# Cross-attention and gated FFN block: activations transposed by SP's DMAs instead of TensorE

## The reference

```
x = x + tanh(g_xattn) * attention(layernorm(x), ctx)   # 32 query heads of width 16, 8 key/value heads
x = x + tanh(g_ffn)   * ffn(layernorm(x))              # 512 -> 1536 -> 512

attention: q = X Wq^T + bq;  k, v = ctx Wk^T + bk, ctx Wv^T + bv
           softmax(q k^T / 4, masked by rows and by padding) v, then Wo, bo
ffn:       (silu(X gate_w * gate_s) * (X up_w * up_s)) down_w * down_s, weights rounded to fp8
```

## Time and profile before

| | |
|---|---|
| median of 3 runs | 626.36 us (625.19 to 628.47) |
| the profiled execution | 625.76 us, span 624.0 us |
| mean granted clock of PE | 0.967 of full |
| busy: PE, DVE, ACT, POOL | 572.9, 494.7, 361.4, 236.6 us |
| DMA | 50.24 MB, mean 81 GB/s |

### The profile page before, as it was taken

One profiled execution on the slowest core, in us unless ns is written; L12 is line 12 of the kernel. 1 busy time (PEld: TensorE's weight loads), 2 busy tenths in 40 slices (PEclk: granted clock), 3 DMA queues, 4 the chain that ended last, 5 costly groups with the idle time before them and its releaser, 6 DMA issues.

```text
span 624.0 us, 14382 instructions
## 1 busy us (share of the span) xinstructions
PE 572.9 (92%) x5165; PEld 358.2 (57%) x5165; DVE 494.7 (79%) x1527; ACT 361.4 (58%) x672; POOL 236.6 (38%) x323
## 2 busy tenths in 40 slices
PE   4747798699999999999999999999998999799997
PEld 4525353357764677457755776467744664466683
DVE  3577667989889999998989988998799888754321
ACT  4453577457674567546664668366755664675361
POOL 3020204020465117630565038611652266038383
PEclk9958899779999999999999999999999999999999
DMA  8683564433021501233121412120323010020000
GB/s 290 210 269 110 162 149 133 122 97 124 14 58 29 177 4 46 69 93 104 29 72 39 124 45 59 49 77 27 79 51 89 3 30 8 19 71 20 17 19 34
DMA packets 53872, 50.24 MB, mean 81 GB/s; under 512 B 7501, under 2 KB 41386, under 8 KB 53802
## 3 DMA queue, kind: packets, MB, share of 16 engines
q1 hardware_dynamic: 53280, 48.72, 26.9%
q10 hardware_dynamic: 522, 0.61, 0.3%
HBM read 35.15 MB, written 9.44 MB: 71 GB/s over the span
## 4 chain that ended last, share of the span: by engine, by line
PE 74%; DVE 15%; issue 4%; DMA 2%; POOL 2%; ACT 1%; SPq 0%; ACTq 0%; POOLq 0%; DVEq 0%
PE work L1178 28%; PE work L1189 10%; PE av L1078 8%; PE work L1109 7%; DVE junk L896 6%; PE sc L1052 6%; PE sc L1068 4%; PE work L1156 4%; DVE ws L905 4%; PE work L1129 2%; PE sc L1064 1%; PE work L1165 1%; PE work L1139 1%; PE work L1118 1%; DVE bst L837 1%
## 5 line engine op out<-in xcount | busy, mean ns | idle before, releaser
L896 DVE CUSTOM_DVE_ANT_0 junk<-sc,mq 128x256 bf16<-128x256 f32 x512 | 186.4, 420 | 40.7 <-PE sc L1052 39.2
L905 DVE SCALAR_TENSOR_TENSOR ws<-sc,padc,mask_k 128x1024 f32<-128x1024 f32 x112 | 143.3, 1280 | 11.8 <-PE sc L1068 9.1
L762 ACT ACTIVATE ws<-ws 128x1024 f32<-128x1024 f32 x112 | 116.2, 1052 | 17.0 <-DVE ws L905 16.8
L691 POOL TENSOR_TENSOR ff<-ga,up 128x256 f32<-128x256 f32 x96 | 69.3, 730 | 113.2 <-DVE ga L986 112.8
L1178 PE MATMUL work<-h_h,wg 128*128 128x256 f16 x384 | 89.6, 274 | 2.0 <-DVE h_l L981 2.0
L1178 PE MATMUL work<-h_h,wu 128*128 128x256 f16 x384 | 89.1, 273 | 0.0
L1178 PE MATMUL work<-h_l,wu 128*128 128x256 f16 x384 | 89.0, 273 | 0.0
L1178 PE MATMUL work<-h_l,wg 128*128 128x256 f16 x384 | 89.0, 273 | 0.0
L698 POOL TENSOR_TENSOR f_l<-ff,f_h 128x256 f16<-128x256 f32 x96 | 63.9, 672 | 56.4 <-ACT f_h L828 56.3
L1189 PE MATMUL work<-wd,f_h 128*128 128x512 fp8e4 x192 | 73.0, 380 | 0.0
L1189 PE MATMUL work<-wd,f_l 128*128 128x512 fp8e4 x192 | 72.8, 379 | 0.0
(11 more groups left out here) (129 smaller groups left out, 1029.9 us busy)
## 6 DMA issues: line engine op xcount, KB each, us to landing
qs<-q_scratch SPq DMA_DIRECT2D x96, 64.0 KB, 2.5
cin<-in_ctx SPq DMA_DIRECT2D x8, 512.0 KB, 4.2
xin<-in_x SPq DMA_DIRECT2D x8, 512.0 KB, 5.4
xb<-in_x SPq DMA_DIRECT2D x8, 512.0 KB, 4.3
att_u<-un SPq DMA_DIRECT2D x128, 32.0 KB, 2.0
out_x<-yt SPq DMA_DIRECT2D x16, 256.0 KB, 2.0
ks<-k_scratch SPq DMA_DIRECT2D x48, 64.0 KB, 2.5
q_scratch<-qh SPq DMA_DIRECT2D x16, 128.0 KB, 2.0
```

Source lines behind the costliest of these rows:

```text
L691: pool.tensor_tensor(ff[:, n % RING, :], ga[:, n % RING, :], up[:, n % RING, :], ALU.mult).then_inc(ff_done, 1)
L762: act.activation(ws[:, unit, :, :], ws[:, unit, :, :], ACT.Exp, scale=1.0 / SSC).then_inc(exp_done, 1)
L896: last = dve.tensor_tensor_reduce(junk[:, j, :], sc[0][:, place(j)], mq[b % 2][:, t, :], 1.0, -3.4e38, ALU.add, ALU.max, mx[:, t, col:col ...
L905: dve.scalar_tensor_tensor(out=ws[:, n % 4, :, :], in0=sc[1][:, :].rearrange("p (j l) -> p j l", j=HPG), scalar=padc[b % 2][:, kt:kt + 1], ...
```

## The change

The three activations are split into high and low halves first, with rows on the partitions, and then each half is transposed by a DMA of SP.

- PE: `xT`, `cT`, `x2T` go, 24 transposes of 128x128 f32 in a batch; with them six uses of the PSUM banks.
- ACT: the cast to the high half now reads the f32 rows in SBUF and writes a row tile (xr_h, cr_h, h2r_h), 128x512, for each half n of the rows.
- POOL: the subtraction to the low half (xr_l, cr_l, h2r_l), six of 128x512 in a batch, in place of DVE's six.
- SP: twelve `dma_start_transpose` of 128x512 f16 in a batch (four each for x, c, x2), from the row tiles into xh, xl, ch, cl, h2_h, h2_l. The low one waits for POOL behind the high one.
- Waits: q waits for x_in, k (and with it v) for c_in, gu for h2_in, each 64 for four transfers. The loads of x and c wait for POOL's subtraction of the batch before. SP waits, before it overwrites xh, ch or h2_h, for the last reader on PE (q 1, v, gu 11 of the batch before).
- Tiles: xn and x2n go; the norms write xin and xb in place, so the residual's load of the next batch waits for x2_low. mask_b and ident_b lie in yt. The factor 4 of ctx goes into Wk.
- All places are set anew. From the second out of batch 3 to its first gu, PE now has

```diff
-IN_BANKS = ("xT", "q", "cT", "k", "v", "spread", "out", "x2T", "gu")
+IN_BANKS = ("q", "k", "v", "spread", "out", "gu")
...
                 if name == "load_x" and b:
-                    sp.wait_ge(normed[0], 2 * b)
+                    sp.wait_ge(x_low, 2 * b)
...
                 if name == "load_xb":
+                    past(sp, x2_low, 2 * b)
+                    sp.dma_start(xb[:, :, :], x_v[b]).then_inc(ld_xb, 16)
+                if name == "xT":
+                    sp.wait_ge(x_high, 2 * b + n + 1)
                     if b:
-                        wait_free(sp, "out", 1, b - 1)
-                    sp.dma_start(xb[:, :, :], x_v[b]).then_inc(ld_xb, 16)
+                        wait_ready(sp, "q", 1, b - 1)
+                    sp.dma_start_transpose(xh[:, :, n * P:(n + 1) * P], xr_h[:, n, :]).then_inc(x_in, 16)
+                    sp.wait_ge(x_low, 2 * b + n + 1)
+                    sp.dma_start_transpose(xl[:, :, n * P:(n + 1) * P], xr_l[:, n, :]).then_inc(x_in, 16)
...
+                if name == "x2T":
+                    pool.wait_ge(x2_high, 2 * b + n + 1)
+                    past(pool, h2_in, 64 * b)
+                    pool.tensor_tensor(h2r_l[:, n, :], xb[:, n, :], h2r_h[:, n, :],
+                                       ALU.subtract).then_inc(x2_low, 1)
...
                 if name == "x2T":
-                    wait_ready(act, name, n, b)
-                    if b:
-                        wait_ready(act, "gu", FT - 1, b - 1)
-                    act.activation(h2_h[:, 2 * n:2 * n + 2, :], halves(bank), ACT.Copy).then_inc(x2_high, 1)
+                    act.wait_ge(normed[1], 2 * b + n + 1)
+                    past(act, h2_in, 64 * b)
+                    act.activation(h2r_h[:, n, :], xb[:, n, :], ACT.Copy).then_inc(x2_high, 1)
...
-                if name == "x2T":
-                    dve.wait_ge(x2_high, 2 * b + n + 1)
-                    dve.tensor_tensor(h2_l[:, 2 * n:2 * n + 2, :], halves(bank), h2_h[:, 2 * n:2 * n + 2, :],
-                                      ALU.subtract).then_inc(freed, 1)
...
                 if name == "gu":
                     if n == 0 and b == 0:
                         pe.wait_ge(f8_done, len(slabs))
                     if n == 0:
-                        for i in range(2):
-                            wait_free(pe, "x2T", i, b)
+                        pe.wait_ge(h2_in, 64 * (b + 1))
```

More of the change, by code:

```diff
@@ L53 @@
 PE_AT = {
[L54 to L60, removed]
@@ L117 @@
[L117 to L125, removed]
+    "pad_row": [3.2532],
+    "padc": [37.6401],
@@ L126 @@
+    "x2T": [98.4415, 99.1556],
 }
 SP_AT = {
[L129 to L139, removed]
+    "load_x": [-200.8497],
+    "load_c": [-188.9527],
+    "load_xb": [-92.1274],
+    "put_q": [-158.3097, -136.9484],
@@ L140 @@
+    "get_q": [-156.1422, -130.376],
+    "rows": [-125.4718, -108.2147],
+    "gather": [-95.302, -92.1126],
+    "store": [-28.1756, -26.6447],
+    "put_k": [-157.9372],
+    "get_k": [-146.8456],
+    "den": [-92.1957],
+    "xT": [-175.9939, -173.1422],
+    "cT": [-170.0178, -168.223],
+    "x2T": [-70.2614, -69.3271],
 }
 PE_FIRST = {
-    "gu": [50.2422, 53.1248, 54.0185, 55.067, 56.535, 58.2144, 58.704, 59.2703, 59.342, 59.8342, 62.2681, 62.4752],
-    "maxima": [-183.727, -50.8962, -23.9023, -17.9854, -17.7211, -17.69, -17.3057, -13.7715, -6.7207, -2.2685,
-               -0.4092, 0.9104, 2.1701, 2.5303, 6.5651, 7.8774],
@@ L208 @@
+    "cT": [-9944.6745, -9903.0438],
+    "x2T": [102.8167, 103.3011],
 }
 SP_FIRST = {
-    "load_xb": [-76.7724],
-    "put_q": [-201.5747, -106.2388],
-    "get_q": [-138.1748, -103.8086],
-    "rows": [-100.2596, -77.6096],
-    "gather": [-70.3549, -50.0156],
-    "store": [-10.7445, -1.7046],
-    "put_k": [-139.0221],
-    "get_k": [-137.4682],
-    "den": [-65.5708],
+    "load_xb": [-126.6719],
+    "put_q": [-154.9186, -142.2669],
+    "get_q": [-148.04, -140.3164],
+    "rows": [-126.827, -104.8412],
@@ L292 @@
+    "cT": [-24.2735, -22.0353],
+    "x2T": [92.3431, 92.938],
 }
 SP_LAST = {
-    "load_x": [-165.1293],
-    "load_c": [-160.3978],
-    "load_xb": [-73.5065],
-    "put_q": [-129.106, -123.6214],
-    "get_q": [-111.2559, -107.6974],
-    "rows": [-105.2968, -81.0932],
-    "gather": [-75.6883, -59.0669],
-    "store": [-40.8265, -40.7234],
-    "put_k": [-138.4836],
-    "get_k": [-125.9663],
-    "den": [-65.2771],
+    "load_x": [-214.721],
+    "load_c": [-204.6784],
+    "load_xb": [-99.5857],
@@ L305 @@
+    "put_q": [-161.6389, -154.4471],
+    "get_q": [-154.2496, -129.2075],
+    "rows": [-124.753, -116.3198],
+    "gather": [-97.8443, -75.8103],
+    "store": [-49.5226, -49.197],
+    "put_k": [-157.672],
+    "get_k": [-153.7618],
+    "den": [-88.4027],
+    "xT": [-172.6298, -168.3597],
+    "cT": [-185.1658, -177.3801],
+    "x2T": [-72.5445, -69.4743],
 }
 SETUP = ["columns", "Wk", "Wq0", "Wq1", "Wq2", "Wq3", "Wv", "mask", "Wo0", "Wo1", "Wo2", "Wo3"]
-SETUP_PE = [-5352.6902, -5349.489, -5174.4074, -5165.6533, -5156.8993, -5139.3911, -4544.8103, -997.1066,
-    -988.8414, -653.6282, -261.8989, -220.8964]
```

469 lines of the change are left out of this document (236 added, 233 removed).

## The result

Twenty executions of the changed kernel on the same chips as twenty of the kernel before: **623.09 us** (621.16 to 629.71) against 627.59 us (625.19 to 633.25), ratio **0.9933, 95% interval 0.9912 to 0.9954** (below, the brackets behind a ratio are this interval). The change gains 0.7% where 2.1% was forecast. The profiled execution took 621.2 us, its span is 619.4 (before 625.76 and 624.0). Single executions of either kernel spread over 8 us, and the kernel before's four longest of the seventeen timed beside e1 to e4 (630.7 to 632.7 us) had a granted clock of 0.951 to 0.957, the other thirteen 0.965 to 0.970.

A forecast was written before the change was run, and what follows sets the result against it. PE was taken to bound the steady state, with the fill setting the pace before. Span 624.0 - 16.2 (transposes) + 2.0 (head) + 1.4 (tail) = 611.2, plus 1.8 around it: 613 us, -2.1%; range 601 to 655.

The forecast's parts named there:

- the head: Start of the run, up to q of batch 0: q at about 21 us instead of 18.71, counted as +2 us.
- SP 0.65, landing 2.5: Price taken for each transposing DMA: 0.65 us of SP's issuing and 2.5 us to landing.
- the 18 fours of the fill: Groups of four PE transposes in the first 147.5 us: counted as nothing, at most 9.7 us.
- Steady state: After 147.5 us: 30 groups of four PE transposes removed at 0.54 us each, 16.2 us; a batch of 64 us.
- What leaves PE's queue shortens a batch one for one: Steady-state batches: PE is busy nearly throughout, so 3.2 us of transposes removed come off each batch.
- DVE not the bound, counted as nothing: VectorE loses six low-half subtractions, 4.1 us a batch, falling from 62 to 58 us; no gain counted.
- Both thresholds: Free room for each transposing DMA in a 64 us batch: 2.5 us of SP's issuing, 4.1 us of the DMA engines.
- rival B: A transposing DMA costs over 2.5 us of SP or 4.1 of the rings: 643 to about 730 us; chance 0.16.
- Tail: Last out to last gate-and-up: x2's transposing takes 10.6 us of latency; gate-and-up at 589.5 instead of 588.08, +1.4 us.
- Delays fuse and fsplit by up to 1.2 us; the ring holds that: GpSimd's six added subtractions, 6.9 us a batch, delay work feeding the down projection; a ring of four tiles absorbs it.
- C: SP, in order, stands at transposes with late GpSimd halves, delaying get_q, rows or gather: 637 to 661 us; chance 0.14.
- D: Waits as long as the removed work, or VectorE holding the period: 624 to 629 us; chance 0.12.

The follow-up runs named there:

- e1: The changed kernel with batch 0's x and context transposed by PE again: 621.18 us, ratio 0.9894 to the kernel before.
- e4: The changed kernel with all 96 transposing DMAs replaced by plain ones of the same bytes (values not the reference's): 615.64 us, ratio 0.9803.
- e6: e1 with the small VectorE instruction that turns variances into ve moved to GpSimd: 615.25 us, ratio 0.9823.
- e5: The changed kernel with the small VectorE instruction that turns variances into ve moved to GpSimd: 620.93 us, ratio 0.9914.
- e12: e5 with only the context of batch 0 transposed by PE, its x staying with SP: 614.3 us, ratio 0.9788.
- e3: The changed kernel with batch 0's eight transposing DMAs replaced by plain ones of the same bytes (operands not transposed): 621.7 us, ratio 0.9897.
- e7: e6 with the last batch's x2 transposed by PE and a down piece back ahead of the last out: 614.12 us, ratio 0.9798.
- e14: e12 with e7's tail (the last batch's x2 transposed by PE): 615.7 us, ratio 0.9811.
- e11: e6 with its 88 transposing DMAs replaced by plain ones of the same bytes (values not the reference's): 611.44 us, ratio 0.9735.
- e15: e14 with its 88 transposing DMAs replaced by plain ones of the same bytes (values not the reference's): 613.03 us, ratio 0.9771.
- e13: The kernel before, old places, without the pieces xT, cT and x2T from batch 2 on (values not the reference's): 618.44 us, ratio 0.9859.
- e8: The kernel before; from batch 2 on each four f32 transposes are one f16 matmul (values not the reference's): 626.0 us, ratio 1.0.
- e2: The changed kernel with loads that batch 0's start doesn't need issued behind its eight transposing DMAs on SP: 631.45 us, ratio 1.0045.
- e9: The kernel before; from batch 2 on VectorE's halves of xT, cT, x2T cut to 2 x 16 columns (values not the reference's): 626.41 us, ratio 0.9969.
- e10: The edits of e8 and e9 together on the kernel before, from batch 2 on (values not the reference's): 622.44 us, ratio 0.9904.

## Why the prediction was wrong

**The step that failed is the head**, as the prediction put it: "q is later by 1 to 2.5 us, I take +2", with "SP 0.65, landing 2.5". Measured: q0 8.5 us later, and gu0 10.2 later. I took x's way as if SP were free when the halves are ready. It was not: the context's four DMAs stood ahead of it, and each took 2.0 to 3.6 us to issue. I had written down that the rings are full, and used it for the landing time alone, while it also governs how long SP's queue stands at each DMA. That this term is most of the miss is shown by e6 against e5: with x and context of batch 0 back on PE the time falls by 5.7 us of the 8.2. With the context alone (e12) it does as well: e6 and e12 run at 615.25 and 614.3 us, ratios 0.9823 and 0.9788, against the forecast's 613 (0.979 of 626.36). Both also have ve on GpSimd; with ve on VectorE the same step gave 2 us (e1). The order of SP's start, with the context ahead of x, was written down with the change; the prediction did not walk through it.

Of the 10.2 us some 8.4 are the late q, carried one for one up to the first maxima (43.0 against 34.6); about 2 more are lost by gu0. For most of these 2 the new order of the fill is not the cause. From the first maxima to gu0 the kernel before takes 112.8 us, 117.2 with the shift of 4.4, at a granted clock of 0.82. Eleven profiled executions share the new order there. Six of them (e3 to e7, e14) had a granted clock of 0.81 to 0.83 and took 117.0 to 118.4 us; five (after, e1, e11, e12, e15) had 0.78 to 0.80 and took 118.9 to 121.3, the kernel after 119.0 at 0.80. So at the clock of the kernel before the new order costs about 1 us at most, and the rest goes with the lower clock, which differs from one execution to the next. What makes it lower is open, and so is why the first maxima of e6 and e12 still come 2.2 us later than before (36.8 against 34.6). What paces the fill is plain in PE's waits, 43 to 79 us (total, times, longest):

```profile
PE sc L1077 <- DVE mx L934: 16.1, 10, 1.9
PE sc L1077 <- DVE wo_l L907: 6.6, 1, 6.6
```

Maxima and PE hand each other one bank, and PE idles 1.7 us in each turn. The prediction gave the 18 fours of the fill no value. No gain appears there: e13 takes eight of them away, and its gu0 is at 148.2 (147.4 before).

**Steady state: right.** 64.9 and 64.2 us in the two batches of the earlier trace rows (64 forecast), PE full, GpSimd 31 to 37 us, VectorE 57 to 60, and 14.8 us from gu0 to gu7, as forecast. "What leaves PE's queue shortens a batch one for one" holds for whole pieces: in the two batches of e13 PE's busy time falls from 67.2 to 64.5 us and the batch from 67.2 or 67.3 to 64.6 (2.7 us, where six fours were put at 3.2). It does not hold for PE time that leaves a bank and a turn in place: e8 gained nothing. "PSUM: six uses fewer, a relief that I don't count" and "DVE not the bound, counted as nothing" were terms of one gain with PE's: thinned alone the pieces are worth 0 (PE) and 1.6 us (VectorE), thinned together 5.6, gone whole 7.8.

**The price of a DMA.** SP's issue 1.26 us (0.65 taken, bounds 0.39 to 2.6; "under 1 us each" was the sign of being right), landing 2.5 us (right), 544 packets (512 guessed), 0.79 us of the rings. The 0.65 is the price of a plain DMA of these rows (0.64 in e4). Both thresholds hold (2.5 and 4.1 us), so rival B does not decide the steady state; in the head it is what happened, smaller than B's 17 us. The estimate from the page "VectorE: DVE Perf Modes" of the Trainium skill, section "The three transpose paths", 5.2 us for a DMA, would have made 680 us; the rows show less than a sixth of it on the rings. That transposing DMAs are as fast as regular ones, as the Trainium skill's page "Advanced Engine Details and Errata", section "X-Bar Transpose (TRN2)", has it, the traces bear out for the landing (2.5 us against 2.4 to 2.6 for x in e4), and not for the issue on SP (1.26 against 0.64) nor quite for the rings (0.79 us each against 0.63 in e4).

**Tail.** +1.4 taken, 2.9 of latency measured, but at most about 1 us of time (e7, within the noise; e14 shows none of it).

**GpSimd.** "Delays fuse and fsplit by up to 1.2 us; the ring holds that" looked only at GpSimd's own consumers. What it missed is the wait of VectorE's smallest instruction for a gap in GpSimd's work: 4.35 us in the profiled execution of e1, 4.36 in that of e4, 1.31 in that of the kernel after. It cost PE 3.7 us in e1; what it costs in the median is not resolved (e5: 1.2 us by the ratios).

**Rivals.** C (a late half holds up SP in order, and others behind it) is the nearest to the truth in kind, in another place: not get_q behind a late half, but x behind the slow context. D's result (624 to 629) misses the median by 1 us, its mechanism did not occur: the removed time came out in full where it was expected.

## What to carry to other kernels

When work moves from a compute engine to a DMA queue, walk through that queue in order from its first instruction, with the issue times that DMAs have while the rings are full, and not with those of a quiet trace. In the first microseconds here the engine was idle and the queue the scarce one, so leave the first batch's (or half of it) on the engine: here that is worth some 6 us (e6 against e5), more than the whole change brought. Remove pieces whole; making them thinner left the bank and the turn, and gave less. When GpSimd is filled up, look at VectorE's smallest instructions.

## What was not expected of the hardware

- The time that a DMA keeps SP's queue depends on what the rings hold: 1.26 us for a 128 KB transposing one, 2.0 to 3.6 us while the first loads run (after), 1.2 to 1.3 us in the same place with fewer loads ahead (e2).
- A plain DMA of the same 128 x 4 runs of 256 bytes took 0.64 us (e4), half of the transposing one, and put_q's 128 KB take 0.39: the size in KB is not the measure.
- A VectorE tensor_scalar on 128x2 f32 took 4.35 us, ending with a run of six GpSimd instructions without a gap; 0.17 us otherwise.
- Where PE and VectorE hand each other single banks, a saving on either side alone hardly shows (0 us in e8, 1.6 in e9), and part of it comes out when both are saved (5.6 us in e10).
- The same order of work, from the first maxima to gu0, took 117.0 us in the execution with the highest granted clock there (0.83, e5) and 121.3 in that with the lowest (0.78, e11).
